# Reordering the openings and the weight change of a two-layer cross-attention kernel, and a centred second query stage

## The reference, cut to what matters

```python
x = x + _L0_xattn_ref(_layernorm(x), ctx_4096, Wq, Wk, Wv, Wo, q_norm_w, k_norm_w)
x = x + _L0_attn_ref(_layernorm(x), ...)       # gated FFN with a Taylor mixer
x = x + _L0_ffn_ref(_layernorm(x), ...)        # low-rank FFN
x = x + _L1_xattn_ref(_layernorm(x), ctx_4096, mask, Wq, Wk, Wv, Wo, q_norm_w, k_norm_w)
x = x + _L1_attn_ref(_layernorm(x), ...)
x = x + _L1_ffn_ref(_layernorm(x), ...)
# cross-attention: q = rms_norm(xn @ Wq) per head of 128; k = rms_norm(ctx @ Wk), v = ctx @ Wv, 8 heads
#   softmax(q k^T / sqrt(128)) v @ Wo, 32 query heads; layer 0 also attends to its own latents
# _layernorm(x) = (x - mean) / sqrt(var + 1e-5);  rms_norm(y) = y * rsqrt(mean(y^2) + eps) * w
```

## Time and profile before

| | us |
|---|---|
| median of 3 runs (lowest, highest) | 1445.07 (1444.0, 1445.44) |
| profiled execution, its own time | 1443.81 |
| its span, first to last instruction | 1442.0 |
| PE busy | 1414.9 (98%) |
| DVE busy | 1021.4 (71%) |
| ACT busy | 844.8 (59%) |
| POOL busy | 361.7 (25%) |

### The profile page before, as it was taken

One profiled execution on the slowest core, in us unless ns is written; L12 is line 12 of the kernel. 1 busy time (PEld: TensorE's weight loads), 2 busy tenths in 40 slices (PEclk: granted clock), 3 DMA queues, 4 the chain that ended last, 5 costly groups with the idle time before them and its releaser, 6 DMA issues.

```text
span 1442.0 us, 24186 instructions
## 1 busy us (share of the span) xinstructions
PE 1414.9 (98%) x7942; PEld 1193.5 (83%) x7942; DVE 1021.4 (71%) x1897; ACT 844.8 (59%) x1476; POOL 361.7 (25%) x542
## 2 busy tenths in 40 slices
PE   8999999999999999999999999999999999999998
PEld 6877888887888888889778788888888888887887
DVE  7988988887666667758668555556755656776765
ACT  5845666656555556736447455556755555773443
POOL 2323323232342424015233322222221212101000
PEclk9999999999999999999999999999999999999999
DMA  7565545566455455347155433335543334342342
GB/s 274 180 234 192 189 161 186 190 220 227 142 188 169 150 163 174 117 183 229 73 178 211 153 125 126 130 118 178 166 134 121 133 123 161 132 183 68 110 159 96
DMA packets 79677, 232.44 MB, mean 161 GB/s; under 512 B 17696, under 2 KB 34848, under 8 KB 72320
## 3 DMA queue, kind: packets, MB, share of 16 engines
q1 hardware_dynamic: 79584, 231.25, 47.1%
HBM read 191.77 MB, written 39.45 MB: 160 GB/s over the span
## 4 chain that ended last, share of the span: by engine, by line
PE 86%; DVE 7%; DMA 2%; ACT 2%; issue 2%; POOL 1%; SPq 0%; DVEq 0%; POOLq 0%; ACTq 0%
PE g_kbanks L54 12%; PE g_kbanks L56 12%; PE g_kbanks L55 12%; PE g_pobanks L1786 8%; PE g_vbank L54 5%; PE g_vbank L55 5%; PE g_vbank L56 5%; PE g_pobanks L1772 4%; PE g_ktbank L1798 3%; PE g_sbank L1754 3%; PE g_sbank L54 2%; PE g_sbank L56 2%; PE g_sbank L55 2%; PE g_pobanks L54 1%; PE g_pobanks L56 1%
## 5 line engine op out<-in xcount | busy, mean ns | idle before, releaser
L54 PE MATMUL g_kbanks<-c_wkv_r,c_cT_r 128*128 128x512 f32 x768 | 311.4, 405 | 4.4 <-ACT c0a_keep L1984 2.1
L56 PE MATMUL g_kbanks<-c_wkv_r,c_cT_r 128*128 128x512 f32 x768 | 302.8, 394 | 0.0
L55 PE MATMUL g_kbanks<-c_wkv_r,c_cT_r 128*128 128x512 f32 x768 | 301.9, 393 | 0.0
L54 PEld LDWEIGHTS g_kbanks<-c_wkv_r,c_cT_r 128*128 128x128 f32 x768 | 144.8, 189 | 35.1 <-DVE c_wkv_r L257 2.7
L56 PEld LDWEIGHTS g_kbanks<-c_wkv_r,c_cT_r 128*128 128x128 f32 x768 | 144.2, 188 | 32.9
L55 PEld LDWEIGHTS g_kbanks<-c_wkv_r,c_cT_r 128*128 128x128 f32 x768 | 144.8, 189 | 27.2
L54 PE MATMUL g_vbank<-c_wkv_r,c_cT_r 128*128 128x512 f32 x256 | 101.1, 395 | 0.0
L55 PE MATMUL g_vbank<-c_wkv_r,c_cT_r 128*128 128x512 f32 x256 | 100.7, 393 | 0.0
L56 PE MATMUL g_vbank<-c_wkv_r,c_cT_r 128*128 128x512 f32 x256 | 100.6, 393 | 0.0
L1674 POOL TENSOR_TENSOR c1a_ms<-c1a_ss,c_const 128x4 f32<-128x4 f32 x64 | 13.7, 214 | 346.3 <-DVE c1a_ss L2101 346.3
L2107 DVE TENSOR_TENSOR c1a_kn<-c1a_kn,c1a_rstd 128x512 f32<-128x512 f32 x64 | 66.7, 1042 | 43.1 <-POOL c1a_rstd L1677 43.1
(11 more groups left out here) (541 smaller groups left out, 3776.2 us busy)
## 6 DMA issues: line engine op xcount, KB each, us to landing
c_cT_r<-ctx_split_dram SPq DMA_DIRECT2D x48, 1024.0 KB, 5.7
c_cT_r<-ctx_split_dram SPq DMA_DIRECT2D x48, 768.0 KB, 4.8
ctx_split_dram<-c_cT_r SPq DMA_DIRECT2D x16, 1792.0 KB, 6.5
c_wkv<-in_l_wo SPq DMA_DIRECT2D x16, 1024.0 KB, 4.9
g_stage<-in_l_wq SPq DMA_DIRECT2D x15, 1024.0 KB, 5.1
e_stage<-in_e_w SPq DMA_DIRECT2D x20, 768.0 KB, 4.2
c_cT<-in_ctx SPq DMA_DIRECT2D x32, 256.0 KB, 3.0
m_stage<-in_mix_ffn SPq DMA_DIRECT2D x10, 768.0 KB, 4.3
```

Of the source, the lines that this page charges most:

```text
L54: nc.tensor.matmul(out, a[0], b[1], start=start, stop=False, skip_group_check=reopen)
L55: nc.tensor.matmul(out, a[0], b[0], start=False, stop=False, skip_group_check=reopen)
L56: return nc.tensor.matmul(out, a[1], b[0], start=False, stop=stop, skip_group_check=reopen)
```

## The change

1. **First opening.** One idle product of 512 columns less; DVE normalises tile 0 ahead of the low part of the first weight chunk; ACT makes the high part of the transposed tile 0 behind the first chunk.
2. **Opening of attention (quads 0 and 1).** Product p3 moves ahead of p4, into the bank `obank`, and the value sum is made in two additions. The key square moves ahead of the copy u2 (early quads), `normalise(2m, 0)` ahead of the context sums, the context's high parts behind the exponential. In layer 1, ACT takes an exponential of a constant in quad 0.
3. **Context sums.** In quads 3 to 14 of layer 0 the four sums are made by POOL, behind its roots, its split of the queries and of the latent keys. ACT's high parts stay ahead of the second `pt_copy`, DVE's low part 0 follows `normalise(2m, 0)`, ahead of the second head's maximum.
4. **Weight change.** SP loads B21 ahead of the latent values' loads; the high parts of B21, T2, T1, T3, T4, B22 move later on ACT, and their low parts on DVE.
5. **End of the low-rank FFN.** PE runs four products of the last third that need only high parts ahead of the low-rank ones; DVE makes the second copy of `l2s` instead of ACT.
6. **Second query stage.** `centre` (x less its mean) replaces `normalise`; POOL's roots of the layer norm go, and the head norm's constant becomes (var + 1e-5) * eps per token (`scaled_eps`).

```diff
@@ context sums: POOL's quad
             else:
                 root(2 * m, 0)
+            if prepared(hf, m + 1) and not early(m):
+                pool.wait_ge(products, all_made(m - 1))
+                context.sums(pool, nc.gpsimd, *following(hf, b, side))
             if tail and par == 0 and side == 1:
                 for i in range(1 + hf):
                     wsums.add(pool, hf, j, i)
@@ DVE's quad
+            normalise(2 * m, 0)
             if prepared(hf, m + 1):
-                if not is_at(m, 0):
-                    dve.wait_ge(products, made(m - 1, "p3"))
-                context.sums(dve, *following(hf, b, side))
-            normalise(2 * m, 0)
-            if prepared(hf, m + 1) and not is_at(u, 0):
-                context.make_lo(dve, *following(hf, b, side), 0)
+                if early(m):
+                    if not is_at(m, 0):
+                        dve.wait_ge(products, all_made(m - 1))
+                    context.sums(dve, nc.vector, *following(hf, b, side))
+                else:
+                    context.make_lo(dve, *following(hf, b, side), 0)
...
+                if early(m):
+                    context.make_lo(dve, *following(hf, b, side), 0)
+                if not is_at(m, 1):
+                    context.make_lo(dve, *following(hf, b, side), 1)
...
+            if is_at(u, 0):
+                dve.wait_ge(products, made(m, "p5"))
+                nc.vector.tensor_tensor(keep[:, 0, :], zbank[:, :], keep[:, 0, :], ALU.add).then_inc(va_part, 1)
+                dve.wait_ge(va_part, m + 1)
+                dve.wait_ge(products, made(m, "p3"))
+                nc.vector.tensor_tensor(v[:, par, 2 * side, :], obank, keep[:, 0, :], ALU.add).then_inc(va_added, 1)
@@ ACT's quad
             divide(x1, k1)
-            if not is_at(u, 0):
+            if not early(m):
                 contexts_hi(hf, b, side, m)
...
-            if turning:
-                kvw.make_hi(act, 1, kvw.B21)
             if turned:
+                kvw.make_hi(act, 1, kvw.T4)
                 kvw.make_hi(act, 1, kvw.B22)
             pt_copy(summed_up(u, par, side, True)[0])
...
             exponential(x2, k2)
+            if early(m):
+                contexts_hi(hf, b, side, m)
             if turning:
-                kvw.make_hi(act, 1, kvw.T2)
+                kvw.make_hi(act, 1, kvw.B21)
@@ PE's quad
             product(hf, side, context.S3, kvw.T3, x_bank, False).then_inc(products, 1)
+            if is_at(u, 0):
+                wait_weights(kvw.B22)
+                if is_at(m, 0):
+                    pe.wait_ge(*border.placed)
+                product(hf, side, context.S4, kvw.B22, obank, True).then_inc(products, 1)
@@ LayerNormSteps
+    def centre(self, dve, t):
+        dve.wait_ge(self.mv_done, t + 1)
+        self.nc.vector.tensor_scalar(self.xn[:, t, :], self.x[:, t, :], self.mv[:, t, 0:1], None,
+                                     ALU.subtract).then_inc(self.normed, 1)
+    def scaled_eps(self, pool, out, t, eps):
+        pool.wait_ge(self.mv_done, t + 1)
+        self.nc.gpsimd.tensor_scalar(out, self.mv[:, t, 1:2].broadcast_to(out.shape), EPS_LN, eps,
+                                     ALU.add, ALU.mult).then_inc(self.eps_added, 1)
@@ second query stage, DVE
             ln.moments(dve, 0)
+            ln.centre(dve, 0)
             lora.add(dve, 1)
-            ln.normalise(dve, 0)
```

More of the change, by code:

```diff
@@ L696, in gpsimd @@
         nc.gpsimd.memset(const[:, 1, :], eps).then_inc(const_set, 1)
-        ln.power(pool)
-        for t in range(TT):
-            ln.root(pool, t)
+        if first:
+            ln.power(pool)
+            for t in range(TT):
+                ln.root(pool, t)
+        else:
+            for t in range(TT):
+                ln.scaled_eps(pool, eps_of[:, t, :], t, eps)
         for n in range(NN):
@@ L765, in scalar @@
             lora.scalar(act, mix, first_tile)
[L766 to L770, removed]
+        if first:
+            stream.make_first_hi(act, 0)
+            ln.make_hi(act, 0)
+            for c in range(1, DC):
+                stream.make_first_hi(act, c)
+            ln.make_hi(act, 1)
+        else:
+            for t in range(TT):
+                ln.make_hi(act, t)
         def square(n):
@@ L1583, in quad @@
         def quad(hf, j, b, par, cycle, u, side, m):
+            turning = is_at(m, PAIRS // 2 - 1)
+            if turning:
+                if tail:
+                    wsums.all_stored(sp, 0)
+                sp.wait_ge(products, made(m, "p1"))
+                kvw.load(sp, 1, kvw.B21)
             if tail and side == 0:
@@ L1604, in quad @@
                 kvw.load(sp, 1, kvw.B11)
[L1605 to L1612, removed]
+            if turning:
+                for name, block in zip(ORDER[1:], range(kvw.T2, kvw.COUNT)):
+                    sp.wait_ge(products, made(m, name))
+                    kvw.load(sp, 1, block)
             if not is_at(u, UNITS - 1):
@@ L1855, in quad @@
                 kt(2 * m, 0)
-            wait_weights(kvw.B22)
-            pe.wait_ge(vb_added, m + 1)
-            product(hf, side, context.S4, kvw.B22, zbank, False).then_inc(products, 1)
+            if not is_at(u, 0):
+                wait_weights(kvw.B22)
+                pe.wait_ge(vb_added, m + 1)
+                product(hf, side, context.S4, kvw.B22, zbank, False).then_inc(products, 1)
         def finish():
@@ L1966, in quad @@
             if early(m):
-                key_square(2 * m, 0, ka_added, m + 1)
+                if is_at(m, 0) and not tail:
+                    act.wait_ge(const_set, 2)
+                    nc.scalar.activation(p[:, 0:UNIT_H], const[:, 0, :], ACT.Exp)
                 if not is_at(m, 0):
@@ L2175, in quad @@
             total(2 * m + 1, 1)
+            if prepared(hf, m + 1) and is_at(m, 1):
+                context.make_lo(dve, *following(hf, b, side), 1)
             if is_at(u, 0):
@@ L2758, in tensor @@
         low_rank(LORA_F - 1)
+        m = LORA_M - 1
+        pe.wait_ge(self.hs_hi, LORA_M)
+        for t in range(TT):
+            for w in reversed(self.dw):
+                nc.tensor.matmul(self.ybank[t][:, :], self.hss[0][:, m, t * P:(t + 1) * P], w[:, m, :],
+                                 start=False, stop=False)
         pe.wait_ge(self.l2_hi, 2)
@@ L2805, in scalar @@
         act.wait_ge(self.l2_zero, 1)
-        for i in range(2):
-            nc.scalar.activation(self.l2s[i * QUAD:i * QUAD + LORA_R, :], self.lbank[0:LORA_R, 0:TOK], ACT.Copy,
-                                 scale=0.5).then_inc(self.l2_hi, 1)
+        nc.scalar.activation(self.l2s[0:LORA_R, :], self.lbank[0:LORA_R, 0:TOK], ACT.Copy,
+                             scale=0.5).then_inc(self.l2_hi, 1)
         split_sum(LORA_M - 1)
```

77 lines of the change are left out of this document (43 added, 34 removed).

## The result

The changed kernel takes 1469.76 us (median of 4 runs, 1468.94 to 1477.17), the kernel before 1444.53 us on the same chip (4 runs, 1443.79 to 1445.44): ratio 1.0183, 95% interval 1.0154 to 1.0213 (each ratio here is the one on record, estimated from all runs; that of the two medians is 1.0175). It is slower by some 25 us. The profiled execution took 1468.94 us, its span is 1467.1 us.

The account below looks back on a forecast made before the run. PE bounds the kernel, busy 1414.9 of 1442.0 us. Terms +25.8 - 3.2 + 1.1 + 2.0 - 2.3 - 1.4 - 1.1 = +20.9 on 1443.8 give 1464.7, as median 1466; forecast 1459 to 1471 (chance 0.66), range 1452 to 1477.

Parts of the forecast that it names:

- The step that decides the sign: Quads 3 to 14, layer 0: sums on POOL delay `pt_copy`; PE waits 3.2 us (side 1), 1.1 (side 0), +25.8.
- The clock: Rival, side-1 quads: PE's six waits of about 3.2 us bring half clock, 10 us more, 1476 us; chance 0.13.
- The signs named for them: Traces to expect: u3 waits and weight change's half clock gone, second query stage's transposes right after the ninth idle product.
- Opening of attention, layer 0: Quads 0 to 2: u3 and most key waits go, but the context comes late; +2.0 us at quad 3's start.
- Weight change: Quads 15 and 16: old wait and half clock go, new split waits come; -3.2 us layer 0, +1.1 layer 1.
- the second one: Layer 0, quad 16: product p7 waits about 1.5 us for T3, of which 0.5 were there before.
- Layer 1's opening: Layer 1's first quads: waits for u3 and keys go, the exponential's table loads earlier; -2.3 us.
- the second query opening: Low-rank FFN's end and second query stage: x complete earlier, POOL's root leaves the chain to the transposes; -1.1 us.
- First opening: Kernel start: DVE normalises earlier, PE's transposes start at 6.1 instead of 8.01 us; -1.4 us stay.
- Hidden: Rival, quads 3 to 14: ACT finds POOL's sums ready, the 25.8 us fall away, 1440 us; chance 0.08.
- Half price: Rival, quads 3 to 14: query split quicker without DVE's sums, DVE's relief helps; +13 instead of 25.8, 1453 us; chance 0.11.

Follow-up runs that it names:

- E1: Changed kernel with the context sums of quads 3 to 14 back on DVE, ahead of normalise: 1437.29 us, ratio 0.9949; repeated 1438.06 us, ratio 0.9950.
- E2: Kernel before with only the context sums of quads 3 to 14 moved to POOL: 1476.65 us, ratio 1.0218.
- E3: Changed kernel, sums still on POOL, ACT's high parts behind the second exponential and DVE's low part 0 behind `ot_place`: 1438.51 us, ratio 0.9957.
- E4: Changed kernel with 24 idle identity transposes on PE ahead of `pv` in side-1 quads 3 to 13: 1462.35 us, ratio 1.0120.
- E5: E1 with the context sums ahead of `normalise` also in quads 0 to 2 of layer 0: 1435.63 us, ratio 0.9935.
- E7: Kernel before with only the weight change's part of the change: 1440.46 us, ratio 0.9966.
- E6: E5 with T2's high part ahead of quad 15's second divide, its low part ahead of quad 16's first normalise: 1434.2 us, ratio 0.9924.

## Why the prediction was right, and which terms were off

**The step that decides the sign held in its mechanism, its places and its size.** Predicted were twelve waits for `pt_copy`, 3.2 us in side-1 and 1.1 us in side-0 quads, 25.8 us in all. The trace has twelve, 25.7 us in all: 3.94 in quad 3, 3.12 to 3.29 in the other five of side 1, 0.92 to 1.03 in side 0. In quad 3 the third sum was to end 2.34 us after the first begins; ACT starts 2.37 us after it (138.68 less 136.31). Only 0.74 us of that first wait is beyond the pattern. One step of the reckoning does not come out as written: for side 0 it takes half of the excess of 2.77 over 1.79 us, and 0.85 + 0.49 is 1.34, not 1.1. The waits, 0.92 to 1.03 us, lie below both, and the quads lose 1.2 to 1.3 us each. The additions take what POOL's rows had foretold:

```profile
L420 POOL TENSOR_TENSOR c_cT<-c_cT x48: 721/734/1067, 136.3 to 337.8; 128x256 f32<-128x256 f32 x48
```

That the cause is the chain sums, high parts, `pt_copy` is shown by removal (E1), alone (E2), and by E3, which leaves the sums on POOL and takes only what stands behind them away.

By the Trainium skill (GPSIMD Engine Reference, Engine selection) GpSimd is about two times slower on such an operation; the runs have 734 ns to DVE's 424, 1.73 times. The factor by itself is not the price: on the slower engine the sums cost some 1.0 us in all (E3 beside E1), once nothing that PE needs stands behind them.

**The clock was a term, not a rival.** I had it apart, as an all-or-nothing case of chance 0.13, six stretches of 1.6 us. It came in part: four stretches in quads 3 to 14, 6.0 us by E4. It is the term that was missing from the sum: 25.7 + 6.0 of the 32.6 us measured. The 0.9 us left are a remainder of small amounts: the six side-0 quads lose 0.25 to 0.29 us each beyond their wait, 1.7 together, and quads 5, 9 and 13 lose 0.3 us less each than their wait and 1.5 us for the clock.

What the other parts of the change cost in quads 3 to 14 is measured apart. E1, with the sums on DVE, loses 0.9 us there, nearly all of it in quad 3 (-0.20 to +0.66), where PE of E1 waits 0.17 us for keys and 0.31 us for `pt_copy` and the kernel before did not. E2, the kernel before with only the sums moved to POOL, loses 31.8, also with four falls of the clock. Together that is 32.7 for the 32.6 measured. In the changed kernel most of those 0.9 us can stand inside the first wait, which is 3.94 us there and 3.29 in E2. I had no term for them, and their cause wasn't tried.

The size of 1.6 us per stretch held (1.5 in E4, 1.5 to 1.6 between E2 and the changed kernel). What failed was the argument against it, that 3.2 us is shorter than the one stretch that had shown a fall. In four of six side-1 quads it was long enough.

By the Trainium skill (TensorE: Matmul & The Clock Gate, Why this matters for your kernels) gaps between bursts drop the clock. The trace now agrees at a gap of 3.13 us (quad 5), where I had only one of 4.03, and quads 7 and 11 (3.16 and 3.12 us) kept the full clock: it is no certainty at this length.

**Smaller terms.** All but one were too pessimistic. The signs named for them are there: no wait for u3 in the openings, the half clock at the weight change gone, and the second query stage's transposes at once behind the ninth idle product (761.75), where PE had stood 0.58 us.

*Opening of attention, layer 0:* +1.1 for +2.0. The mechanism is there (the context's low part late, 0.49 us ahead of quad 1 and 2.66 ahead of quad 2; E5), and E4, whose opening runs at full clock, has the parts: quad 1 starts 0.25 us earlier against before, where I had 0.2 later; quad 2 loses 0.9 us, as reckoned; quad 3 loses 0.45, where I had 0.9. In the changed kernel the half clock makes the second part 2.1 us, and quad 3 gives 0.8 back.

*Weight change:* -4.3 in layer 0 for -3.2, +0.45 in layer 1 for +1.1; E7 alone gives the same. The new waits were to be 0.9 and 1.5 us and are these:

```profile
367.50 0.47 PE L54 MATMUL g_vbank<-c_wkv_r,c_cT_r 128*128 128x512 f32 x1 [0.74 <-issue]
370.03 0.50 PE L54 MATMUL g_kbanks<-c_wkv_r,c_cT_r 128*128 128x512 f32 x1 [0.90 <-DVE c_wkv_r L257]
```

The term that was mis-sized is the second one. PE goes on 2.53 us after T1's low part released it, which is DVE's unbroken work up to the end of T3's, and p5 fills 1.63 of them; the wait for T3 is the difference, however late T1 was. E6 shows the same: the first wait falls to 0.20 us and the second keeps its size.

*Layer 1's opening and the second query opening:* -2.8 for -2.3, -1.6 for -1.1, both inside their bounds; nothing was run on them.

*First opening:* -0.7 for -1.4. The transposes start at 6.16 us, where I had 6.1, and the first product at 8.19 instead of 10.05; most of these 1.9 us are lost again before quad 0. Eight other profiles have this opening or the old one: -0.7 to -1.3 at quad 0 with the new one (six), 0.0 and -0.5 with the old (two). One profile doesn't settle its size.

The sum: the steps outside quads 3 to 14 came out 2.6 us better than forecast, quads 3 to 14 came out 6.8 us worse. That is the 4.2 us between +20.9 and +25.1. That the two errors went opposite ways is luck, and it is part of why the median, 1469.76 us, still fell inside the forecast's 1459 to 1471: with the small terms as reckoned it would have been some 1472.

**The rivals.** "Hidden" falls by the twelve waits; E1's 1437.3 us is about what it would have given (1440). "Half price" falls: the query split took 1.30 instead of 1.38 us, and POOL was not free for the sums before 136.3 in quad 3. The longest of the four runs, 1477.17 us, is also the one with the lowest mean clock, 0.988 for 0.994.

## What to carry to other kernels

Moving work to an idle engine is judged by what stands behind its result in the queue of the engine that takes it: here a step 1.7 times slower cost 25.7 us in PE's waits and, with its two followers moved behind the urgent copy, some 1.0 us. Repeated waits of about 3 us on PE want the clock's price on top: here 6.0 us on the 19.8 of the six side-1 quads; but nothing in the opening, where E4 at full clock lost the same 1.1 us. And when two waits of one engine for the same other engine follow each other, don't reckon them one by one: as long as the first is there, the second is what the other engine has to do between the two releases less what the waiting one has to do, here 2.5 less 1.6 us, and pulling both forward leaves it as it is.

## What was not expected of the hardware

The length of an idle stretch did not decide whether the clock fell. After a wait of 2.66 us at the same place it was at 0.50 in the changed kernel, in both profiles of E1 and in E3, and at 1.00 in E4. Of the changed kernel's six waits of 3.1 to 3.9 us, four were followed by half clock, beginning 0.4 to 1.1 us after PE had gone on; in E2, with six of 3.1 to 3.3 us in the same quads, it was again four, in quads 3, 7, 11 and 13 instead of 3, 5, 9 and 13. E2 also has a stretch behind the old wait at the weight change and one at 738 us that no other kernel has:

```profile
738.00:741.30 3.30, 3.30 (x17) 3.30 (x17) 1.40 (x3) 0.77 (x2) 0.00 (x0) 0.50 0.02 5
```

The four runs of the changed kernel had clocks of 0.994 three times and 0.988 once, and that one was 7 to 8 us longer; reckoned at 1.5 us each that would be some five stretches more, an estimate, as that run has no profile. What makes the clock fall in one run and not in the next stays open.
